# The layer norm of a graph layer on one core: groups turned back in 32x32 squares by VectorE in place of 128x128 transposes on TensorE

## The reference

```python
h = item_feat @ W_item.T + b_item        # 10000 x 128
b = x @ W_user.T + b_user                # 10000 x 128
z = x + relu(adj @ h + b)                # adj: 10000 x 10000, float32
out = (z - mean(z)) / sqrt(var(z) + 1e-5)   # over the 128 features of each row
```

## Time and profile before

| | before |
|---|---|
| median of 3 runs | 1103.01 us (1102.78 to 1103.82) |
| the profiled execution's own time | 1102.25 us |
| its span, first to last instruction | 1100.5 us |
| TensorE busy | 1089.7 us, 99% |
| VectorE busy | 944.2 us, 86% |
| ScalarE busy | 807.5 us, 73% |
| GpSimd busy | 57.8 us, 5% |
| moved by DMA | 417.15 MB, 379 GB/s over the span |

### The profile page before, as it was taken

The page is one execution under the profiler, slowest core; times in us unless marked ns, Lnnn a source line. Parts: engine busy times, 40 slices in busy tenths (PEclk is TensorE's granted clock), DMA queues, the critical chain, the costliest instruction groups (busy, mean ns, idle before and its releaser), DMA issues. The chain is left out here.

```text
span 1100.5 us, 14565 instructions
## 1 busy us (share of the span) xinstructions
PE 1089.7 (99%) x5009; PEld 908.1 (83%) x5009; DVE 944.2 (86%) x682; ACT 807.5 (73%) x584; POOL 57.8 (5%) x29
## 2 busy tenths in 40 slices
PE   8999999999999999999999999999999999999997
PEld 7878888888888888888888888888888888888887
DVE  6889988888888888888888888888888888888876
ACT  5677877777777777777777777676767777777765
POOL 5870000000000000000000000000000000000000
PEclk9999999999999999999999999999999999999999
DMA  9999999999999999999999999999999999999996
GB/s 344 371 361 408 390 423 388 387 391 398 373 404 372 403 376 376 404 395 371 389 385 403 374 381 395 393 379 395 383 387 385 386 388 393 381 393 379 396 265 198
DMA packets 76324, 417.15 MB, mean 379 GB/s; under 512 B 8784, under 2 KB 19328, under 8 KB 30224
## 3 DMA queue, kind: packets, MB, share of 16 engines
q1 hardware_dynamic: 76160, 416.75, 97.8%
q10 hardware_dynamic: 144, 0.13, 0.0%
HBM read 411.67 MB, written 5.18 MB: 379 GB/s over the span
## 5 line engine op out<-in xcount | busy, mean ns | idle before, releaser
L505 DVE TENSOR_TENSOR adj_lo<-adj,adj_hi 128x2048 fp32r<-128x2048 f32 (+2 forms) x399 | 868.9, 2192 | 112.5 <-ACT adj_hi L380 110.0
L380 ACT CAST adj_hi<-adj 128x2048 fp32r<-128x2048 f32 (+2 forms) x399 | 731.1, 1833 | 261.7 <-PE acc L321 212.7
L315 PE MATMUL acc<-adj_hi,h_hi 128*128 128x512 f32 (+1 forms) x1580 | 608.2, 386 | 1.6 <-ACT adj_hi L386 1.6
L316 PE MATMUL acc<-adj_hi,h_lo 128*128 128x512 f32 (+1 forms) x1580 | 604.9, 384 | 0.0
L321 PE MATMUL acc<-adj_lo,h_hi 128*128 128x512 f32 (+1 forms) x1580 | 419.6, 385 | 0.8 <-DVE adj_lo L512 0.6
L315 PEld LDWEIGHTS acc<-adj_hi,h_hi 128*128 128x128 f32 x1580 | 296.8, 188 | 59.6 <-POOL h_lo L467 1.7
L316 PEld LDWEIGHTS acc<-adj_hi,h_lo 128*128 128x128 f32 x1580 | 296.9, 188 | 57.5
L321 PEld LDWEIGHTS acc<-adj_lo,h_hi 128*128 128x128 f32 x1580 | 292.5, 188 | 61.6 <-DVE adj_lo L505 2.3
L467 POOL TENSOR_TENSOR h_lo<-h_full,h_hi 128x512 fp32r<-128x512 f32 (+1 forms) x20 | 53.7, 2690 | 21.6 <-ACT h_hi L394 21.3
L523 DVE BATCH_NORM_STATS2 stats<-z_ps 128x6 f32<-128x128 f32 x79 | 17.6, 286 | 29.2 <-PE z_ps L331 29.2
L415 ACT ACTIVATE items<-z_ps,shift,rstd 128x128 f32<-128x128 f32 x79 | 29.7, 457 | 0.4 <-DVE shift L541 0.4
(11 more groups left out here) (31 smaller groups left out, 63.4 us busy)
## 6 DMA issues: line engine op xcount, KB each, us to landing
adj<-adj_t SPq DMA_DIRECT2D x360, 1024.0 KB, 7.4
adj<-adj_t SPq DMA_DIRECT2D x21, 512.0 KB, 5.4
adj<-adj_narrow SPq DMA_DIRECT2D x19, 544.0 KB, 5.3
items<-item_t SPq DMA_DIRECT2D x19, 256.0 KB, 4.7
xg<-x_t SPq DMA_DIRECT2D x19, 256.0 KB, 4.5
out<-items SPq DMA_DIRECT2D x19, 256.0 KB, 7.4
tail_in<-adj_tail SPq DMA_DIRECT2D x57, 32.0 KB, 4.1
adj<-adj_narrow SPq DMA_DIRECT2D x1, 272.0 KB, 3.8
```

The lines of the kernel that those rows point to most:

```text
L315: nc.tensor.matmul(into, h_hi[:, k, :], adj_hi[:, s, c, 0:u], start=(k == 0), stop=False)
L316: nc.tensor.matmul(into, h_lo[:, k, :], adj_hi[:, s, c, 0:u], start=False, stop=False)
L380: nc.scalar.copy(adj_hi[:, s, start:, 0:u], adj[:, a, start:, 0:u]).then_inc(hi_made, 1)
L505: nc.vector.tensor_tensor(adj_lo[:, s, start:, 0:u], adj[:, a, start:, 0:u], adj_hi[:, s, start:, 0:u].bitcast(F32), ALU.subtract).then_in ...
```

## The change

For the first 19 groups the turn is no longer made by TensorE. VectorE turns `z_t` in squares of 32x32 (one instruction on 128x512, t = 6), so that row 32n + i of the group stands on partition 32q + i for features 32q to 32q + 31, as 16 stretches n of 32 values: each row's 128 features lie on four partitions, a quarter (q) on each. The sum over a row is then made in three steps: VectorE reduces each stretch of 32 (`part`, 128x16, t = 7), ScalarE copies the four bands of 32 partitions side by side (`gathered`, four instructions on 32x16, t = 8), and VectorE adds the four (`total`, 32x16, t = 9). ScalarE writes minus the mean back to the four bands (four instructions, t = 10), GpSimd adds it (128x512), ScalarE squares (128x512, t = 12), and the sums of the squares go the same way (t = 13, 14, 15). ScalarE takes the root (t = 15), VectorE the reciprocal (t = 16), ScalarE spreads it (four instructions, t = 17), and GpSimd multiplies (128x512). Its product lies where the normalised block lay, and the store waits for it. The last group keeps the old way, in its own output tensor. The output of the 19 groups leaves in the turned layout and is put in order on the host. To make room, `h_full` now lies where `h_lo` lies, and GpSimd subtracts in place; the chunk left over has a small buffer of its own, `h_tail`, which VectorE fills by an instruction of its own at the last tile of `h`.

The diff, cut to its core (buffers, semaphores, the last group's renamed functions and the host's reshaping are left out):

```diff
-TURN_AT = 7
-STATS_AT, MOMENTS_AT = 8, 9
-STD_AT = 11
-RSTD_AT, SHIFT_AT = 12, 13
-NORM_AT = 15
+TURN_AT = 6
+SUM_AT = 7
+GATHER_SUMS_AT = 8
+TOTAL_AT = 9
+SPREAD_MEAN_AT = 10
+SQUARE_AT = 12
+SUM_SQUARES_AT = 13
+GATHER_SQUARES_AT = 14
+TOTAL_SQUARES_AT = 15
+STD_AT = 15
+RSTD_AT = 16
+SPREAD_RSTD_AT = 17
...
+        with nc.sbuf_tensor("h_full", [P, USER + 1, HID], F32) as h_full:
+            pass
         h_lo = sb("h_lo", [P, USER + 1, HID], F32R)
         h_pack = sb("h_pack", [P, HID], F32R)
-        h_full = sb("h_full", [P, H_RING, PER_TILE, HID])
...
-        normed = items[:, 1, :].rearrange("p (b n) -> p b n", b=BLOCKS)
+        z_b = items[:, 1, :].rearrange("p (n j) -> p n j", j=SQ)
+        normed_last = items[:, 1, :].rearrange("p (b n) -> p b n", b=BLOCKS)
+        centred = items[:, 2, :].rearrange("p (n j) -> p n j", j=SQ)
+        squares = items[:, 3, :].rearrange("p (n j) -> p n j", j=SQ)
...
             def store(g):
                 sp.wait_ge(out_ready, g + 1)
-                n = blocks(g)
-                sp.dma_start(out[g, :, 0:n, :], normed[:, 0:n, :]).then_inc(out_stored, 16)
+                if isinstance(g, int) and g == GROUPS - 1:
+                    n = blocks(g)
+                    sp.dma_start(out_last, normed_last[:, 0:n, :]).then_inc(out_stored, 16)
+                else:
+                    sp.dma_start(out[g], items[:, 1, :]).then_inc(out_stored, 16)
 
...
             def turn_back(g):
 
                 pe.wait_ge(z_added, g + 1)
-                if later(g, 1):
-                    pe.wait_ge(out_ready, g)
                 for b in range(blocks(g)):
                     mm = nc.tensor.transpose(z_ps[:, b, :], z_t[:, b * P:b * P + P], ident[:, :])
                 mm.then_inc(z_turned, 1)
...
                 for t in range(TILES):
-                    if t == TURN_AT:
-                        turn_back(g - 1)
...
-            def deviation(g):
-                act.wait_ge(moments_done, g + 1)
+            def gather(n):
+                act.wait_ge(summed, n)
+                if later(n, 2):
+                    act.wait_ge(totalled, n - 1)
+                for q in range(QUADS):
+                    ins = nc.scalar.copy(gathered[:, q, :], part[q * SQ:q * SQ + SQ, :])
+                ins.then_inc(gathered_in, 1)
+            def spread_mean(g):
+                act.wait_ge(totalled, 2 * g + 1)
+                if later(g, 1):
+                    act.wait_ge(centred_made, g)
+                for q in range(QUADS):
+                    ins = nc.scalar.mul(minus_mean[q * SQ:q * SQ + SQ, :], total[:, :], -1.0 / HID)
+                ins.then_inc(mean_spread, 1)
+            def square(g):
+                act.wait_ge(centred_made, g + 1)
+                if later(g, 1):
+                    act.wait_ge(summed, 2 * g)
+                nc.scalar.activation(squares, centred, ACT.Square).then_inc(squared, 1)
+            def deviation_32(g):
+                act.wait_ge(totalled, 2 * g + 2)
+                if later(g, 1):
+                    act.wait_ge(rstd_32_done, g)
+                nc.scalar.activation(std_32[:, :], total[:, :], ACT.Sqrt, bias=eps[0:SQ, 0:1],
+                                     scale=1.0 / HID).then_inc(std_32_done, 1)
+            def spread_rstd(g):
+                act.wait_ge(rstd_32_done, g + 1)
+                if later(g, 1):
+                    act.wait_ge(out_ready, g)
+                for q in range(QUADS):
+                    ins = nc.scalar.copy(rstd_all[q * SQ:q * SQ + SQ, :], rstd_32[:, :])
+                ins.then_inc(rstd_spread, 1)
+            def deviation_last():
+                act.wait_ge(moments_done, 1)
                 nc.scalar.activation(std[:, :], moments[:, :, 1], ACT.Sqrt, bias=eps[:, 0:1]).then_inc(std_done, 1)
 
-            def normalise(g):
-                act.wait_ge(shift_done, g + 1)
-                if later(g, 1):
-                    act.wait_ge(out_stored, 16 * g)
+            def normalise_last(g):
+                act.wait_ge(shift_done, 1)
+                act.wait_ge(out_stored, 16 * g)
                 for b in range(blocks(g)):
-                    ins = nc.scalar.activation(normed[:, b, :], z_ps[:, b, :], ACT.Identity,
+                    ins = nc.scalar.activation(normed_last[:, b, :], z_ps[:, b, :], ACT.Identity,
                                                bias=shift[:, b:b + 1], scale=rstd[:, b:b + 1])
                 ins.then_inc(out_ready, 1)
...
+                    if t == GATHER_SUMS_AT:
+                        gather(2 * (g - 1) + 1)
+                    if t == SPREAD_MEAN_AT:
+                        spread_mean(g - 1)
+                    if t == SQUARE_AT:
+                        square(g - 1)
+                    if t == GATHER_SQUARES_AT:
+                        gather(2 * (g - 1) + 2)
                     if t == STD_AT:
-                        deviation(g - 1)
-                    if t == NORM_AT:
-                        normalise(g - 1)
+                        deviation_32(g - 1)
+                    if t == SPREAD_RSTD_AT:
+                        spread_rstd(g - 1)
...
+            def centre_and_scale(g):
+                pool.wait_ge(z_turned, g + 1)
+                pool.wait_ge(mean_spread, g + 1)
+                if later(g, 1):
+                    pool.wait_ge(out_ready, g)
+                nc.gpsimd.tensor_tensor(centred, z_b, minus_mean[:, :, None].to_broadcast([P, BANDS, SQ]),
+                                        ALU.add).then_inc(centred_made, 1)
+                pool.wait_ge(centred_made, g + 1)
+                pool.wait_ge(rstd_spread, g + 1)
+                nc.gpsimd.tensor_tensor(z_b, centred, rstd_all[:, :, None].to_broadcast([P, BANDS, SQ]),
+                                        ALU.mult).then_inc(out_ready, 1)
...
+            centre_and_scale(0)
+            with pool.Fori(1, LOOP_PAIRS + 1) as i:
+                centre_and_scale(2 * i - 1)
+                centre_and_scale(2 * i)
+            centre_and_scale(GROUPS - 3)
+            centre_and_scale(GROUPS - 2)
...
             def add_item_bias(t):
-                n = full_chunks(t) + (1 if t == LAST else 0)
-                s = t % H_RING
-                if t >= H_RING:
-                    dve.wait_ge(h_lo_made, t - H_RING + 1)
+                n = full_chunks(t)
+                k = t * PER_TILE
                 dve.wait_ge(h_product, t + 1)
-                nc.vector.tensor_tensor(h_full[:, s, 0:n, :], h_ps[t % H_PS_RING][:, 0:n, :],
+                if t == LAST:
+                    nc.vector.tensor_tensor(h_tail[:, :], h_ps[t % H_PS_RING][:, n, :], bias_item[:, :], ALU.add)
+                nc.vector.tensor_tensor(h_full[:, k:k + n, :], h_ps[t % H_PS_RING][:, 0:n, :],
...
+            def turn(g):
+                dve.wait_ge(z_added, g + 1)
+                if later(g, 1):
+                    dve.wait_ge(out_stored, 16 * g)
+                nc.vector.transpose(items[:, 1, :], z_t).then_inc(z_turned, 1)
+            def sum_bands(g):
+                dve.wait_ge(z_turned, g + 1)
+                if later(g, 1):
+                    dve.wait_ge(gathered_in, 2 * g)
+                nc.vector.tensor_reduce(part[:, :], z_b, mybir.AxisListType.X, ALU.add).then_inc(summed, 1)
+            def sum_square_bands(g):
+                dve.wait_ge(squared, g + 1)
+                dve.wait_ge(gathered_in, 2 * g + 1)
+                nc.vector.tensor_reduce(part[:, :], squares, mybir.AxisListType.X, ALU.add).then_inc(summed, 1)
+            def total_sums(g):
+                dve.wait_ge(gathered_in, 2 * g + 1)
+                if later(g, 1):
+                    dve.wait_ge(std_32_done, g)
+                nc.vector.tensor_reduce(total[:, :], gathered[:, :, :].rearrange("p q n -> p n q"),
+                                        mybir.AxisListType.X, ALU.add).then_inc(totalled, 1)
+            def total_squares(g):
+                dve.wait_ge(gathered_in, 2 * g + 2)
+                dve.wait_ge(mean_spread, g + 1)
+                nc.vector.tensor_reduce(total[:, :], gathered[:, :, :].rearrange("p q n -> p n q"),
+                                        mybir.AxisListType.X, ALU.add).then_inc(totalled, 1)
+            def reciprocal_32(g):
+                dve.wait_ge(std_32_done, g + 1)
+                if later(g, 1):
+                    dve.wait_ge(rstd_spread, g)
+                nc.vector.reciprocal(rstd_32[:, :], std_32[:, :]).then_inc(rstd_32_done, 1)
...
-                    if t == MOMENTS_AT:
-                        aggregate(g - 1)
+                    if t == TURN_AT:
+                        turn(g - 1)
+                    if t == SUM_AT:
+                        sum_bands(g - 1)
+                    if t == TOTAL_AT:
+                        total_sums(g - 1)
+                    if t == SUM_SQUARES_AT:
+                        sum_square_bands(g - 1)
+                    if t == TOTAL_SQUARES_AT:
+                        total_squares(g - 1)
```

(60 more changed lines are left out.)

31 lines of the change are left out of this document (12 added, 19 removed).

## The result

| | before | with the change |
|---|---|---|
| median of 7 runs | 1103.62 us (1102.78 to 1104.88) | 1098.66 us (1096.88 to 1100.47) |
| ratio to before | 1 | 0.9959, 95% interval 0.9950 to 0.9969 |
| the profiled execution's own time | 1102.25 us | 1098.09 us |
| its span | 1100.5 us | 1096.1 us |

A forecast was written before the change was run, and what follows sets the result against it. TensorE's matmul pace was taken as the bound. From the profiled 1102.25 us, minus 8.6 for the turns, plus 0.4 start and 2.2 end, gave 1096.2; plus 0.76 to the median, 1097.0 us, range 1093.8 to 1101.5.

The forecast's parts named there:

- The turn's price: Middle groups: four transposes and the restart cost TensorE 0.48 us a group; 18 turns removed gain 8.6 us.
- VectorE's and ScalarE's new work: Middle groups: VectorE some 47.4 us busy of 53.95, ScalarE about 43; neither becomes a bound.
- GpSimd, 2.94 us each and 0.6 us on VectorE: Two GpSimd instructions per group, 2.94 us each, each delaying VectorE 0.6 us: VectorE at 48.6 of 53.95 us.
- The new waits: Middle groups, t = 8 to 17: adj_lo of tile 18 2.3 to 2.9 us later, cushion 5.7; cost 0.
- so it is made up before t = 5: After the chain, ScalarE has 0.8 us and VectorE 0.5 to spare per tile, so the lag is recovered.
- 4.3 us less than TensorE needs: Loads in the middle: a group's 21.07 MB takes 49.6 us to move, 4.3 less than TensorE needs.
- The full cushion: Tile 15 of a middle group: adj_lo is ready 5.7 us before TensorE comes to it; smaller delays cost nothing.
- The DMA engines hardly run dry: SyncE's queue, held by the store: tile 2's load 2 to 5 us late, up to two loads still in flight.
- Rival 1's point: Waits at t = 13 to 17 use up every group's cushion, from a lag of 6.2 us; slower, chance 0.05.
- The start, 0.4 us: Group 1, whose cushion isn't full: the chain at t = 15 costs between nothing and 2 us, taken as 0.4.
- The end, 2.2 us: Last, narrow group: new steps from t = 14 to 17 cost between 0 and 4.5 us, taken as 2.2.
- Rival 4: The end costs nothing because ScalarE's waits for loads cover the chain: 1094 to 1095 us, chance 0.12.

The follow-up runs named there:

- e_std16: The changed kernel with only the root one tile later (STD_AT 16 in place of 15): 1095.57 us, 0.9933 of the kernel before.
- e_store4: The changed kernel with the store two places later in SyncE's queue (STORE_AT 4 in place of 2): 1096.00 us, 0.9939 of the kernel before.
- the second profile: The changed kernel run and profiled once more, with nothing altered; the profiled execution's own time is 1099.27 us.
- e_spaced: The changed kernel with four VectorE steps (total, sum of squares, their total, reciprocal) one tile earlier: 1094.97 us, 0.9919 of the kernel before.
- e_burden_after: The changed kernel with three idle 128x512 copies on ScalarE behind cast 16 of each group from 1 on: 1111.43 us, one run.

## Why the prediction was right, and where it wasn't

The time was right, 1098.7 in a range from 1093.8 to 1101.5, 1.7 us above the 1097.0 of the sum. Its largest term was right too, and it was right that the loss is at the end. The picture of the middle was wrong, and that it cost nothing there was luck.

- **The turn's price, 0.48 us, gain 8.6 us.** Measured: 53.95 us from mark to mark in 15 of the 18 middle groups, and 8.4 us for all. The number came from the matmuls' own pace, not from the 0.60 us of the transposes' row.
- **VectorE's and ScalarE's new work.** The turn takes 0.704 us and the two sums 0.675 and 0.673, where the add's 0.684 was taken; the sums over bands 0.246 (taken 0.2); four small copies 0.85 (taken 1.0). Rows by shape, with the change:

```profile
L618 DVE STREAM_TRANSPOSE items<-items 128x512 f32<-128x512 f32 x19 | 13.4, 704 | 0.0
...
L624 DVE TENSOR_REDUCE part<-items 128x16 f32<-128x512 f32 x19 | 12.8, 675 | 0.0
...
L635 DVE TENSOR_REDUCE total<-gathered 32x16 f32<-32x64 f32 x19 | 4.7, 246 | 0.0
```

- **GpSimd, 2.94 us each and 0.6 us on VectorE.** It takes 1.97 to 2.26 us in wide groups and 1.06 in the narrow one. Each of the 38 instructions starts while VectorE is in a subtraction, and each ends 0.91 to 0.93 us after that subtraction's end, whether 0.12 us of it were left (narrow group) or 1.35. So it looks as if GpSimd stands until VectorE is through and then needs 0.9 us. The next subtraction, which starts before GpSimd's end, takes 2.35 us, 2.62 at most, in place of 2.29: 0.05 to 0.3 us, not 0.6. The mean over all 360 hides this, 2298 ns against the 2295 of the earlier trace rows. The Trainium skill's rule that the two exclude each other for a whole instruction (SBUF — State Buffer, Who interferes with whom) fits this. It cost VectorE little here because for most of GpSimd's 0.9 us VectorE stood waiting for a cast anyway (0.71 us in the rows below). Two subtractions and GpSimd's instruction between them in group 11, then GpSimd's in the last group:

```profile
667.94 2.22 DVE L598 TENSOR_TENSOR adj_lo<-adj,adj_hi 128x2048 fp32r<-128x2048 f32 x1
...
669.04 2.03 POOL L561 TENSOR_TENSOR items<-items,rstd_all 128x512 f32<-128x512 f32 x1 [18.09 <-ACT rstd_all L469]
...
670.87 2.35 DVE L598 TENSOR_TENSOR adj_lo<-adj,adj_hi 128x2048 fp32r<-128x2048 f32 x1 [0.71 <-ACT adj_hi L409]
...
1084.52 1.05 POOL L561 TENSOR_TENSOR items<-items,rstd_all 128x512 f32<-128x512 f32 x1 [11.71 <-ACT rstd_all L469]
```

- **The new waits.** Their sizes were right: 2.5 us at t = 15, 0.7 at t = 17, both shown above. The step that failed is the next sentence, "so it is made up before t = 5". It counted what ScalarE and VectorE have to spare in a tile (0.8 and 0.5 us), and forgot that a tile can only be made up if it has landed, and that its load is issued when VectorE is done with the tile five before. A late subtraction makes a late load. The loads were costed apart, at 49.6 us a group, "4.3 us less than TensorE needs", and that was true of the DMA engines when they are always asked. They weren't: 360 GB/s in the half of the group with the chain, 423 in the other. The cushion was 0.05 to 1.2 us at tile 16 and 0.3 to 1.3 at tile 18, where 2.8 to 3.4 was predicted, and e_std16 and e_store4 show that either of its two causes can be taken away. The full cushion was also 5.5 us at tile 15 of the kernel before, not the 5.7 worked out. The cost in the middle was 0.2 us all the same, 0.8 in the second profile (971.4 and 972.0 against e_std16's 971.1): TensorE came to the parts just behind them, and nothing in the prediction says why it should have.
- **"The DMA engines hardly run dry"** while the queue is held failed in the same way: alone it would have been right (e_spaced, held as long, has its cushion), behind the late tiles it wasn't. This goes by what they moved; their busy share stayed at 98% (last section).
- **Rival 1's point, a lag of 6.2 us.** The copies' 1.6 us more already cost 0.7 us a group (e_burden_after), at a lag of 3.9 to 4.5 by the prediction's count. The chance of 0.05 was too low for a kernel that stood so near to it.
- **The start, 0.4 us.** The term was for the chain in group 1, whose cushion isn't full. It measured nothing: `adj_lo` of tile 16 was 1.4 us early there (0.6 in the second profile), and group 1 took 54.05 us, 0.1 over the middle, as it did in the kernel before (54.54 against 54.43) and, but for the kernel with the three copies, in every variant with the new middle (54.04 to 54.07). What the prediction didn't have, the rebuilt group 0, measured 1.0003 (0.9994 to 1.0012).
- **The end, 2.2 us.** Measured 3.0 and, against the second profiles, 3.8. The term was sized for the steps from t = 14 to 17 alone, and there it was right: in tiles 14 to 19 TensorE took 2.0 us more than in the kernel before. But it lost 1.6 us already between t = 7 and 11, at the first gather and the spread of the mean, because the group was entered without a cushion: e_store4 has the same steps there, came with 3.3 us in hand, and lost 0.1. Against these stand some 0.5 us for the turn, which went from this group too; the prediction hadn't counted it. ScalarE from t = 8 to 15:

```profile
1067.25 0.84 ACT L440 COPY gathered<-part 32x16 f32<-32x16 f32 x4 [1.19 <-DVE part L624]
...
1070.74 0.89 ACT L448 ACTIVATE minus_mean<-total 32x16 f32<-32x16 f32 x4 [0.51 <-DVE total L635]
...
1077.24 0.85 ACT L440 COPY gathered<-part 32x16 f32<-32x16 f32 x4 [0.96 <-DVE part L629]
...
1080.73 0.31 ACT L461 ACTIVATE std<-total,eps 32x16 f32<-32x16 f32 x1 [1.51 <-DVE total L641]
```

- **Rival 4**, an end that costs nothing, describes e_spaced (31.5 us against 31.6 and 31.3), not the change: the loss was in where the steps stood.

## What to carry to other kernels

When a step of one engine waits for a step that another engine has behind the same tile, and that engine can only start the tile when the first is done with it, the wait is the other's whole work on the tile, 2.5 us here; one constant moved by one was worth 3 us here, beside a gain of 5 from the change itself. A cushion is only worth what refills it: follow a delay round the whole loop (cast, subtraction, free slot, load, landing) before you say that it is made up, and test it by adding a known idle cost and looking where it shows. A busy share of 99% on the bounding engine, and the right period in the middle, are the same with 5 us in hand as with 0.05.
